# Sparse first FFN of a macaron block: routing by whole rows, blocks in plain f32, router stationary, weight stores in an early tick

## The chip, the cores and the metric

The kernel runs on one core of one Trainium2 chip. The metric is the device time of one execution in microseconds, as the median of three runs; lower is better. Times inside the kernel are read from one profiled execution, counted from the start of its span.

## What is computed

The reference is a macaron block on x of shape 8 x 1024 x 256 in f32: a mixture-of-experts FFN, an attention, and the same FFN again (same weights), each behind a layer norm and added to x (the FFNs at half weight).

```python
x = x + 0.5 * ffn(layernorm(x))      # the "first FFN": all of the change is here
x = x + attn(layernorm(x))           # window attention + 256 routed tokens of each row
x = x + 0.5 * ffn(layernorm(x))

def ffn(x):                          # 8 experts, top 2, hidden width 128
    w = softmax(x @ router_w + router_b)
    w2, i2 = top_k(w, 2);  w2 = w2 / sum(w2)
    h = gelu(x @ W1[e] + b1[e])      # 256 -> 128
    return sum over the two of w2 * (h @ W2[e] + b2[e])
```

## The kernel before

"Row" means one of the 8 batch rows of 1024 tokens (8 tiles of 128 tokens); a "group" is half a row (4 tiles), 16 groups in all.

**The first FFN is sparse.** For each group, `group_stats`, `rstd` (with an index of 0), `group_norm` normalise the tokens; `group_turn` transposes them with TensorE (8 transposes, line 812); `group_logits` makes the router's logits with the tokens as the stationary operand (line 822); `group_route` ranks the experts on VectorE; `group_spots` counts places (TensorE, lines 830 and 832, then VectorE); `exp2nd_a` and `group_gates` give the two weights. Then `send` on GpSimd (line 1889) scatters every token tile twice, once for each of its two experts, to `spots_d` in HBM: 8 indirect DMAs a group, 128 in all. Rows are taken in three batches, (0,1), (2,3,4), (5,6,7). When all tokens of a batch lie at their places, SyncE writes pads (`pads`, line 590, 8 DMAs of 256 KB), and the batch is worked off in blocks of 256 tokens of one expert: 23, 31 and 31 blocks, 85 "steps".

**A step** is `block_load` (line 602, 256 KB), `block_turn` (4 transposes, line 842), `block_hi` and `block_lo` (ScalarE line 1148 and VectorE line 1504: the value split in a rounded part and a rest, both fp32r), `w1_copy` (ScalarE, the expert's W1 in both parts), `block_hidden` (6 fp32r matmuls of 256 columns), `block_gelu` (ScalarE, twice: lines 1157 and 1158), `block_hl` (GpSimd line 1893: the rest of h), `block_out` (6 fp32r matmuls of 256 columns), `block_left` (VectorE line 1516, bias), `block_store` (line 608, 256 KB). `mm3` (lines 717 to 719) makes the product of two split operands by three fp32r matmuls.

**The order is written by hand in ticks.** Every engine runs through the same ticks and does what falls in each in program order; an engine that waits holds all its later ticks. Step s starts in tick 24 + s; `block_hidden` is 2 ticks later, `block_out` 5, `block_store` 7. Groups start at ticks `GROUP_AT`, sends are 8 to 11 ticks later, two in a tick. In the third batch's ticks row 0 of the attention is prepared: `fetch` gathers its results, then `combine`, norms and transposes.

**After the ticks** come "slots" of the attention (40 for a row) and then the second FFN, dense; these also use the split weights, which are stored to HBM (`w1_d`, `w2_d`, `b2_d`, 4 MB, line 660) in tick 90 and read back near the end. The three last projections of the change's region, `qkv` of row 0, run in the last ticks.

Of the kernel before, what the change touches and what calls it, by code (L numbers as in the profile page):

```python
# [8 lines left out]
F32 = mybir.dt.float32  # L9
# [9 lines left out]
P = 128  # L19
# [16 lines left out]
BLK = 256  # L36


def build(nc, x_in, gamma_h, wq_h, wkv_h, wo_h, ln_g, ln_b, wqkv, wo_l, rt_q, rt_kv,
# [22 lines left out]
    MAXM = 4 * T * max(r1 - r0 for r0, r1 in BATCH) // 2  # L62
# [7 lines left out]
    with ctx:  # L70
# [56 lines left out]
        home = sb("home", [P, GROUPS, 2, TG], U32)  # L127
        share = sb("share", [P, GROUPS, 2, TG])
# [21 lines left out]
        w2_st = at("w2_st", [P, E, D], F32, yr_off + n1 * 4)  # L150
# [32 lines left out]
        chosen = [sb(f"chosen{i}", [P, TG + 1, E], BF16) for i in range(2)]  # L183
        lg = sb("lg", [P, TG, E])
        lrank = sb("lrank", [P, TG, E])
        l2nd = sb("l2nd", [P, TG, E])
        cmp_g = sb("cmp_g", [P, TG, E, E], BF16)
        cmp_e = sb("cmp_e", [P, TG, E, E], BF16)
        run = sb("run", [P, E])
        sums = sb("sums", [P, TG, E])  # L190
        picks = sb("picks", [P, 2, TG, E])

        spot_f = sb("spot_f", [P, GROUPS, 2, TG])
        spot = sb("spot", [P, GROUPS, 2, TG], U32)
# [14 lines left out]
        xin = [sb(f"xin{i}", [P, BT, D]) for i in range(4)]  # L209
        w1_s = sb("w1_s", [P, E, 2, C, FF], F32R)  # L210
        w1_now = [sb(f"w1_now{i}", [P, 2, C, FF], F32R) for i in range(2)]
        w2_s = [sb("w2_hi", [P, E, D], F32R), sb("w2_lo", [P, E, D], F32R)]
        assert top[0] >= z2 + (HC * N + HC * PADDED + (T + 1) * INNER) * 4
        b2_s = sb("b2s", [64 + E, D], F32R)

        wqkv_st = at("wqkv_st", [P, C, 3 * INNER], F32, top[0])
        b2_st = at("b2_st", [E, D], F32, top[0] + n3 * 4)
        hf = [sb(f"hf{i}", [P, BLK]) for i in range(NH)]
        hl = [sb(f"hl{i}", [P, BLK], F32R) for i in range(NH)]
        hh = [sb(f"hh{i}", [P, BLK], F32R) for i in range(NH)]  # L220
        yout = [sb(f"yout{i}", [P, BT, D]) for i in range(4)]
        block_e = [sb(f"block_e{n}", [P, MAXB], I32) for n in range(len(BATCH))]
        block_row = [sb(f"block_row{n}", [P, MAXB], I32) for n in range(len(BATCH))]
        pad_row = [sb(f"pad_row{n}", [P, E], I32) for n in range(len(BATCH))]
        assert top[0] <= xf_off, (top[0], xf_off)

        xb_off = [xt_off + i * TG * D * 4 for i in range(4)] + [y_off, y_off + TG * D * 4] + [yr_off + (T * (D + 1) + i * TG * D) * 4 for i in range(2)]
        xb = [at(f"xb{i}", [P, TG, D], F32, off) for i, off in enumerate(xb_off)]
        zeros = at("zeros", [P, BT, D], F32, xt_off + 4 * TG * D * 4)
        assert 4 * TG * D + BT * D <= 2 * C * PADDED  # L230
        x_off = [x1_off + T * D * 4, x1_off + (T * D + 2 * C * BLK) * 4, yr_off]
        xh = [at(f"xh{i}", [P, C, BLK], F32R, x_off[i]) for i in range(3)]
        xl = [at(f"xl{i}", [P, C, BLK], F32R, x_off[i] + C * BLK * 4) for i in range(3)]
# [41 lines left out]
        s_xa, s_sc = [sem(f"xa_ld{i}") for i in range(8)], [sem(f"sent{i}") for i in range(8)]  # L275
        s_ax, s_ra, s_exa, s_pos, s_tab, s_zero = sem("xa_turned"), sem("route_a"), sem("exp2_a"), sem("spots"), sem("table"), sem("pads")
        s_home, s_b2all = sem("homes"), sem("b2_all")

        s_bld, s_bst = [sem(f"block_ld{i}") for i in range(4)], [sem(f"block_st{i}") for i in range(4)]
        s_bT, s_bhi, s_blo, s_w1c, s_bh = sem("block_turned"), sem("block_hi"), sem("block_lo"), sem("w1_copied"), sem("block_hidden")  # L280
        s_bge, s_bhl, s_bo, s_by, s_spare = sem("block_gelu"), sem("block_h_lo"), sem("block_out"), sem("block_y"), sem("spare_zero")
# [37 lines left out]
        def group_at(tau, after):  # L319

            return [k for k, t in enumerate(GROUP_AT) if t + after == tau]
# [8 lines left out]
        def batch_of_group(k):  # L330
            return [n for n, (r0, r1) in enumerate(BATCH) if r0 <= k // 2 < r1][0]

        def last_of_batch(k):
            return k == 2 * BATCH[batch_of_group(k)][1] - 1
# [14 lines left out]
        QKV0 = {STEP0 + STEPS + 3 + i: i for i in range(3)}  # L349
# [139 lines left out]
        def left(job):  # L489

            kind, x, i = job
            if kind == "aT":
                return s_ax, 2 * x + i + 1
# [63 lines left out]
        def sent(engine, n):  # L557

            for k in range(2 * BATCH[n][0], 2 * BATCH[n][1]):
                engine.wait_ge(s_sc[k % 8], 128 * (k // 8 + 1))  # L560
# [8 lines left out]
        def sp_program():  # L569
# [7 lines left out]
            def group_load(k):  # L577
                if k in (6, 7):

                    sp.wait_ge(s_wlo, 4)  # L580
                if k >= 8:
                    sp.wait_ge(s_sc[k % 8], 128 * (k // 8))
                sp.dma_start(xb[k % 8][:, :, :], half(x_v, k)).then_inc(s_xa[k % 8], 16)
# [40 lines left out]
            group_load(0)  # L624
            sp.dma_start(rw_st[:, :, :], router_w.rearrange("(c p) n -> p c n", p=P)).then_inc(s_wld[0], 16)
            group_load(1)
# [3 lines left out]
            group_load(2)  # L630
            group_load(3)
            for tau in range(TICKS):
                for s_ in step_at(tau - 7):
                    block_store(s_)
                for s_ in step_at(tau + 3):
                    block_load(s_)
                for k in group_at(tau + 6, 0):
                    if k >= 4:
                        group_load(k)
                if tau == 7:  # L640
                    sp.dma_start(wqkv_st[:, :, :], wqkv.rearrange("(c p) n -> p c n", p=P)).then_inc(s_wld[4], 16)
                if tau == 11:
                    sp.dma_start(b2_all[:, :, :].rearrange("p e n -> p (e n)"), b2.rearrange("(a e) n -> a (e n)", a=1).broadcast_to([P, E * D])).then_inc(s_b2all, 16)
                if tau in (13, 36, 60):

                    if tau == 13:
                        sp.wait_ge(s_const, CONST)
                    n = (13, 36, 60).index(tau)
                    sp.dma_start(spots_d[n][SPARE[n]:SPARE[n] + (E - 1) * BLK, :].rearrange("(j p s) d -> p j (s d)", p=P, s=BT),
                                 zeros[:, :, :].rearrange("p s d -> p (s d)").unsqueeze(1).broadcast_to([P, E - 1, BT * D])).then_inc(s_spare, 16)  # L650
                if tau == 82:
                    sp.dma_start(wqh_s[:, :, :], wq_h.rearrange("(c p) n -> p c n", p=P)).then_inc(s_late, 16)
                    sp.dma_start(wkvh_s[:, :, :], wkv_h.rearrange("(c p) n -> p c n", p=P)).then_inc(s_late, 16)
                if tau == 86:
                    sp.dma_start(wol_s[:, :, :], wo_l.rearrange("(c p) n -> p c n", p=P)).then_inc(s_late, 16)
                    sp.dma_start(woh_s[:, :, :], wo_h.rearrange("(c p) n -> p c n", p=P)).then_inc(s_late, 16)
                if tau == 90:
# [6 lines left out]
                if tau == 70:  # L664
                    attn_load(0, x_v)
            sp.wait_ge(s_bh, STEPS)
# [48 lines left out]
        def pe_program():  # L715
# [11 lines left out]
            def ffn_turn(k, pr):  # L727
                pe.wait_ge(s_norm[0], 2 * (GROUPS + k) + pr + 1)
# [77 lines left out]
            def group_turn(k, pr):  # L806
# [8 lines left out]
            def group_logits(k):  # L815
                pe.wait_ge(s_ax, 2 * k + 2)
                if k == 0:
                    pe.wait_ge(s_wld[0], 16)
# [1264 lines left out]
```

## Time and profile before

| | us |
|---|---|
| median of 3 runs | 2117.42 (2114.1 to 2122.3) |
| profiled execution | 2120.96, its span 2119.2 |
| busy in the span | PE 1892.2, VectorE 1473.1, ScalarE 1214.2, GpSimd 1208.1 |
| mean granted TensorE clock | 0.969 |
| first block load of the three batches | 86.75, 183.36, 288.07 |
| last block store issued | 393.1 |

How to read it: the first FFN takes the time up to about 393 us and the change touches nothing behind that. So what moves the time is when the last step is done. Busy shares over the whole span say little here, since attention and second FFN (four fifths of the time) run behind other limits.

### The profile page before, as it was taken

The page shows a single profiled execution, that of the slowest core. Times are in us where ns is not written, and L with a number is a line of the kernel's source. Part 1 is how long each engine was busy: PE and PEld are TensorE (multiplying, and loading weights), DVE is VectorE, ACT ScalarE, POOL GpSimd, SP SyncE. Part 2 cuts the span into 40 slices and gives each one's busy share as a digit, 9 for nine tenths or more (in the row PEclk, how much of TensorE's full clock was granted, in tenths as well). Part 3 has the DMA queues.
Part 4 walks back from the last instruction along what each step waited for, and adds up shares of the span by engine and source line. Part 5 has one row for each costly group of instructions (what it writes and reads, how often), then busy time and mean ns, then how long its engine had stood idle before and what let it go on. Part 6 is the DMA issues. An engine that isn't in the chain of part 4 may idle for free.

```text
span 2119.2 us, 39516 instructions
## 1 busy us (share of the span) xinstructions
PE 1892.2 (89%) x12240; PEld 1458.9 (69%) x12240; DVE 1473.1 (70%) x5026; ACT 1214.2 (57%) x3005; POOL 1208.1 (57%) x1376
## 2 busy tenths in 40 slices
PE   4568877888998998998998998998999999999998
PEld 4567766655665665665665665665676688888887
DVE  5566856765684685685684684685665488888887
ACT  4356757646556556556556556556555555555554
POOL 6887855284386386385385386386364444444444
PEclk9978988989999999999999999999999999999999
DMA  7567887320031031030030031031023111111110
GB/s 251 172 223 264 269 301 258 119 74 12 6 103 28 8 101 29 9 103 26 20 91 26 9 100 28 9 100 29 4 58 115 37 41 41 39 34 39 40 33 29
DMA packets 106695, 173.74 MB, mean 82 GB/s; under 512 B 13408, under 2 KB 65016, under 8 KB 105592
## 3 DMA queue, kind: packets, MB, share of 16 engines
q1 hardware_dynamic: 83448, 118.42, 17.0%
q0 software_dynamic: 20736, 52.52, 8.0%
q8 instruction: 101, 1.65, 0.3%
q10 hardware_dynamic: 2304, 0.28, 0.2%
q14 instruction: 106, 0.87, 0.1%
HBM read 80.33 MB, written 90.84 MB: 81 GB/s over the span
## 4 chain that ended last, share of the span: by engine, by line
PE 45%; DVE 17%; POOL 12%; issue 11%; ACT 8%; DMA 5%; SPq 1%; DVEq 0%; ACTq 0%; POOLq 0%
PE bank L717 8%; PE bank L719 6%; PE bank L718 6%; PE bank L1000 4%; PE bank L989 4%; PE bank L960 4%; PE bank L971 4%; PE bank L931 3%; POOL spots_d L1889 3%; ACT prob L1277 2%; DVE st L1366 2%; POOL prob L1940 2%; DVE x L1529 2%; DMA z_row<-made_d,home 2%; PE bank L962 1%
## 5 line engine op out<-in xcount | busy, mean ns | idle before, releaser
L1940 POOL TENSOR_TENSOR prob<-prob,rden 128x512 f32<-128x512 f32 x320 | 338.0, 1057 | 456.1 <-DVE rden L1735 452.5
L1277 ACT ACTIVATE prob<-prob,nmax 128x256 f32<-128x256 f32 x512 | 255.9, 502 | 404.1 <-DVE nmax L1717 404.1
L1717 DVE CUSTOM_DVE_ANT_0 prob<-bank,mask 128x256 f32<-128x256 f32 x512 | 195.3, 418 | 103.6 <-PE bank L960 102.5
L1604 DVE SCALAR_TENSOR_TENSOR xb<-bank,gate,xb 128x256 f32<-128x256 f32 x512 | 211.8, 476 | 55.5 <-PE bank L719 54.7
L960 PE MATMUL bank<-kT,qT 64*128 64x256 f32 x1024 | 212.5, 433 | 22.8 <-DVE nmax L1717 22.2
L1865 POOL TENSOR_TENSOR hl<-hf,hh 128x512 fp32r<-128x512 f32 x128 | 164.9, 1294 | 113.4 <-ACT hh L1098 108.8
L971 PE MATMUL bank<-ident,prob 128*128 128x128 f32 x1280 | 199.6, 279 | 19.6 <-POOL prob L1940 19.6
L971 PEld LDWEIGHTS bank<-ident,prob 128*128 128x128 f32 x1280 | 155.0, 143 | 78.5 <-POOL prob L1940 31.0
L1729 DVE COPY probT<-bank 128x512 f32<-128x512 f32 x160 | 110.1, 688 | 120.6 <-PE bank L971 119.8
L1097 ACT ACTIVATE hf<-bank,b1s 128x512 f32<-128x512 f32 x128 | 88.2, 689 | 171.6 <-PE bank L719 168.1
L989 PE MATMUL bank<-probT,V 128*64 128x128 f32 x2048 | 170.2, 287 | 8.2 <-ACT oT_s L1293 6.6
L1927 POOL DMA_INDIRECT hs_d<-yr,place x128 | 130.0, 1016 | 43.6 <-issue 32.3
L960 PEld LDWEIGHTS bank<-kT,qT 64*128 64x128 f32 x1024 | 94.4, 187 | 86.7 <-issue 44.1
L989 PEld LDWEIGHTS bank<-probT,V 128*64 128x64 f32 x2048 | 108.6, 137 | 63.5 <-issue 61.4
L717 PE MATMUL bank<-w,hh 128*128 128x256 f32 x512 | 146.0, 285 | 3.9 <-POOL hl L1865 2.7
L1889 POOL DMA_INDIRECT spots_d<-xb,spot x128 | 127.6, 997 | 34.2 <-issue 32.2
L719 PE MATMUL bank<-w,hh 128*128 128x256 f32 x512 | 144.5, 282 | 0.0
L718 PE MATMUL bank<-w,hl 128*128 128x256 f32 x512 | 144.2, 282 | 0.0
L1000 PE MATMUL bank<-wol,oT_s 128*128 128x256 f32 x512 | 127.3, 392 | 1.2 <-ACT xf_t L1224 1.2
L1749 DVE TENSOR_TENSOR x<-bank,x 128x256 f32<-128x256 f32 x64 | 27.0, 423 | 145.1 <-PE bank L1000 145.1
L717 PE MATMUL bank<-xt_hi,wqkv_hi 128*128 128x512 f32 x256 | 115.5, 451 | 0.0
L1000 PEld LDWEIGHTS bank<-wol,oT_s 128*128 128x128 f32 x512 | 93.0, 191 | 24.1 <-issue 13.8
(254 smaller groups left out, 5461.5 us busy)
## 6 DMA issues: line engine op xcount, KB each, us to landing
xin<-spots_d SPq DMA_DIRECT2D x85, 256.0 KB, 4.1
made_d<-yout SPq DMA_DIRECT2D x85, 256.0 KB, 3.7
xb<-in_L_attn_x SPq DMA_DIRECT2D x16, 512.0 KB, 6.3
x<-in_L_attn_x SPq DMA_DIRECT2D x8, 1024.0 KB, 6.5
x_d<-x SPq DMA_DIRECT2D x8, 1024.0 KB, 4.5
xb<-x_d SPq DMA_DIRECT2D x16, 512.0 KB, 3.8
out<-xb SPq DMA_DIRECT2D x16, 512.0 KB, 2.9
spots_d<-zeros SPq DMA_DIRECT2D x24, 256.0 KB
```

Of the source, the lines that this page charges most:

```text
L717: pe.matmul(o, w[0], x[0], start=start, stop=False)
L718: pe.matmul(o, w[1], x[0], start=False, stop=False)
L719: return pe.matmul(o, w[0], x[1], start=False, stop=stop)
L960: ins = pe.matmul(bank[g % NS][:, 0:KEYS], qT[hs, hp, t * P:(t + 1) * P], kT[hs, hp, t * P:t * P + KEYS], start=True, stop=True)
L971: ins = pe.transpose(bank[3 + j % 2][:, (2 * h + kk) * P:(2 * h + kk + 1) * P], prob[j % NP][:, h, kk * P:(kk + 1) * P], ident[:, :])
L989: ins = pe.matmul(bank[5][h * DH:(h + 1) * DH, hp * P:(hp + 1) * P], V[:, t + kk, hs] if t < T else hv[:, kk, hs], probT[j % 2][:, 2 * h + ...
L1000: ins = pe.matmul(bank[tb][:, 0:D], oT_s[:, ch, :], w[:, ch, :], start=(ch == 0), stop=(ch == HC - 1))
L1277: act.activation(prob[j % NP][:, h, :], src, ACT.Exp, bias=nmax[:, j % 4, h:h + 1], scale=-1.0 if light else 1.0, accum_out=den[:, j % 4, ...
L1604: dve.scalar_tensor_tensor(out=x, in0=bank[ob][:, (t % 2) * D:(t % 2 + 1) * D], scalar=gate[:, k % 2, t, e:e + 1], in1=x, op0=ALU.mult, op ...
L1717: ins = dve.tensor_tensor_reduce(prob[j % NP][:, h, :], bank[g % NS][:, 0:KEYS], mask[:, which, :], -1.0, 3e38, ALU.add, ALU.min, nmax[:, ...
L1889: pool.indirect_dma_start(spots_d[batch_of_group(k)], bass.IndirectOffsetOnAxis(spot[:, k, c, q:q + 1], 0), xb[k % 8][:, q, :], None).then ...
L1940: pool.tensor_tensor(prob[j % NP][:, :, :], prob[j % NP][:, :, :], rden[:, j % 4, :].unsqueeze(2).broadcast_to([P, 2, KEYS]), ALU.mult).th ...
```

## The change

Four edits, with the ticks laid out anew around them.

1. Routing by whole rows: `row_stats`, `row_rstd`, `row_norm`, `row_turn`, `row_route`, `row_exp`, `row_gates`, `row_spots` take 8 tiles at a time, each with half as many instructions on operands of twice the width; the number of sends stays at 128, three in a tick. Rows start at ticks `ROW_AT`; the load of a row is one DMA of 1 MB (row 0 in two halves).
2. The blocks in plain f32: no split of x, h or the weights, so `block_lo`, `block_hl` and one of the two gelus go, `w1_copy` copies half as much, and `block_hidden` and `block_out` have 2 plain matmuls each for 6. The pipeline of a step is two ticks shorter.
3. Logits with the router stationary: 4 matmuls of 512 columns into 8 partitions for a row (`row_logits`), copied by ScalarE and turned back by 8 small transposes.
4. The splits of the weights (still needed by attention and second FFN) move from ticks 2 to 19 to ticks 8 to 25; the store of the split weights moves from tick 90 to tick 18, the loads of the attention's late weights from ticks 82 and 86 to 100 and 106.

```diff
-        STEP0 = 24
-        TICKS = STEP0 + STEPS + 8
-        GROUP_AT = (0, 3, 6, 9, 12, 15, 18, 22, 26, 30, 36, 41, 46, 51, 56, 61)
+        STEP0 = 26
+        TICKS = STEP0 + STEPS + 6
+        ROW_AT = (0, 6, 12, 19, 26, 36, 46, 56)
...
-            jobs = [("aT", k, pr) for k in group_at(tau, 3) for pr in range(2)]
-            jobs += [("alg", k, 0) for k in group_at(tau, 4)]
-            jobs += [("apos", k, 0) for k in group_at(tau, 6)]
+            jobs = [("aT", r, i) for i in range(4) for r in row_at(tau, 4 + i // 2)]
+            jobs += [("alq", r, i) for r in row_at(tau, 6) for i in range(2)]
+            jobs += [("alg", r, 0) for r in row_at(tau, 7)]
+            jobs += [("apos", r, 0) for r in row_at(tau, 9)]
...
-                if tau == 90:
+                if tau == 18:
                     sp.wait_ge(s_wlo, 6)
                     sp.dma_start(w1_d, ...)
...
+                for c in range(C):
+                    ins = pe.matmul(bank[tb][0:E, :], rw_st[:, c, :], xa[h][:, c, :], start=(c == 0), stop=(c == C - 1))
...
+                for t in range(T):
+                    ins = pe.transpose(bank[tb][:, t * E:(t + 1) * E], lgT[t // TG][:, t % TG * P:(t % TG + 1) * P], ident[0:E, 0:E])
...
                 for c in range(C):
-                    ins = mm3(bank[2 + s_ % 2][:, 0:BLK], [w1_now[s_ % 2][:, n, c, :] for n in range(2)], [x[s_ % 3][:, c, :] for x in (xh, xl)],
-                              start=(c == 0), stop=(c == C - 1))
+                    ins = pe.matmul(bank[2 + s_ % 2][:, 0:BLK], w1_now[s_ % 2][:, c, :], xh[s_ % 3][:, c, :], start=(c == 0), stop=(c == C - 1))
...
                 for j in range(BT):
-                    cs = slice(j * P, (j + 1) * P)
-                    ins = mm3(bank[4 + s_ % 2][:, j * D:(j + 1) * D], [hh[s_ % NH][:, cs], hl[s_ % NH][:, cs]], w, start=True, stop=True)
+                    ins = pe.matmul(bank[4 + s_ % 2][:, j * D:(j + 1) * D], hf[s_ % NH][:, j * P:(j + 1) * P], w, start=True, stop=True)
...
-                act.activation(hf[s_ % NH][:, :], bank[2 + s_ % 2][:, 0:BLK], ACT.Gelu, bias=b1_e)
-                act.activation(hh[s_ % NH][:, :], bank[2 + s_ % 2][:, 0:BLK], ACT.Gelu, bias=b1_e).then_inc(s_bge)
+                act.activation(hf[s_ % NH][:, :], bank[2 + s_ % 2][:, 0:BLK], ACT.Gelu, bias=b1_s[:, bass.ds(e_act[s_], 1)]).then_inc(s_bge)
...
                 for s_ in step_at(tau):
                     block_turn(s_)
-                for s_ in step_at(tau - 5):
+                for s_ in step_at(tau - 3):
                     block_out(s_)
-                for s_ in step_at(tau - 2):
+                for s_ in step_at(tau - 1):
                     block_hidden(s_)
...
-                for s_ in step_at(tau - 4):
-                    block_hl(s_)
-                for k in group_at(tau, 1):
-                    rstd(0, k, 2 * k)
-                for k in group_at(tau, 6):
-                    exp2nd_a(k)
-                for i in range(8):
-                    for k in group_at(tau, 8 + i // 2):
-                        send(k, i)
+                for r in row_at(tau, 2):
+                    row_rstd(r)
+                for r in row_at(tau, 9):
+                    row_exp(r)
+                for i in range(2 * T):
+                    for r in row_at(tau, 11 + i // 3):
+                        send(r, i)
```

## Rows read from the trace of the kernel before

**Rows 1.** Windows: us; busy (count) PE, PEld, DVE, ACT, POOL; clock, DMA share, GB/s.

```profile
86.75:183.36 96.61, 71.84 (x471) 68.38 (x471) 62.75 (x201) 58.07 (x119) 79.72 (x99) 0.84 0.70 235
183.36:288.07 104.71, 81.14 (x617) 77.26 (x617) 76.86 (x205) 69.81 (x149) 76.84 (x96) 0.90 0.81 272
288.07:393.50 105.43, 83.10 (x567) 76.00 (x568) 65.55 (x147) 74.00 (x161) 59.98 (x86) 0.89 0.76 261
393.50:2119.20 1725.70, 1615.44 (x10389) 1201.31 (x10387) 1217.05 (x4256) 980.94 (x2521) 929.63 (x995) 0.98 0.15 45
```

**Rows 2.** Timeline of SyncE's queue: start, us, instruction, count.

```profile
86.75 2.81 SPq L602 DMA_DIRECT2D xin<-spots_d  x4
...
172.44 8.01 SPq L590 DMA_DIRECT2D spots_d<-zeros  x8
183.36 0.36 SPq L602 DMA_DIRECT2D xin<-spots_d  x1
...
288.07 0.35 SPq L602 DMA_DIRECT2D xin<-spots_d  x1
...
331.28 0.46 SPq L660 DMA_DIRECT2D w_d<-w_s  x1
```

**Rows 3.** Groups of GpSimd, 86.75 to 183.36: busy, mean ns, idle before, releaser.

```profile
L1889 POOL DMA_INDIRECT spots_d<-xb,spot x52 | 51.3, 987 | 14.5 <-issue 12.7 <-DVE spot L1450 1.7
L1893 POOL TENSOR_TENSOR hl<-hf,hh 128x256 fp32r<-128x256 f32 x20 | 15.2, 764 | 0.9 <-ACT hh L1158 0.5
L1840 POOL TENSOR_TENSOR tri<-tri,cols 128x4 f32<-128x4 f32 x5 | 5.3, 1070 | 0.0
```

**Rows 4.** What TensorE waited for: groups, 86.75 to 393.5; then waits, 86.75 to 183.36.

```profile
L842 PE MATMUL bank<-ident,xin 128*128 128x128 f32 x340 | 61.9, 313 | 43.9 <-DMA xin<-spots_d 25.7 <-DVE xl L1504 18.1
L717 PE MATMUL bank<-w_hi,hh 128*128 x170 | 60.5, 356 | 20.3 <-POOL hl L1893 16.7 <-issue 1.6 <-DVE yout L1516 1.0
...
PE bank L717 <- POOL hl L1893: 10.1, 2, 7.8
PE bank L842 <- DVE xl L1504: 6.7, 5, 4.1
```

**Rows 5.** Timeline of TensorE in an undisturbed tick of the third batch.

```profile
381.49 0.60 PE L842 MATMUL bank<-ident,xin 128*128 128x128 f32 x4
...
382.16 0.28 PE L719 MATMUL bank<-w_lo,hh 128*128 x1
382.28 0.28 PE L717 MATMUL bank<-w_hi,hh 128*128 x1
...
383.35 0.60 PE L842 MATMUL bank<-ident,xin 128*128 128x128 f32 x4
```

**Rows 6.** Timeline of TensorE in the attention: plain f32 matmuls of 256 columns.

```profile
813.10 1.99 PE L1000 MATMUL bank<-wol,oT_s 128*128 128x256 f32 x8
814.93 0.49 PE L971 MATMUL bank<-ident,prob 128*128 128x128 f32 x3
```

**Rows 7.** Timeline of ScalarE in the same ticks.

```profile
382.32 0.46 ACT L1157 ACTIVATE hf<-bank,b1s 128x256 f32<-128x256 f32 x1
...
384.18 0.46 ACT L1157 ACTIVATE hf<-bank,b1s 128x256 f32<-128x256 f32 x1
```

**Rows 8.** Timeline of TensorE's jobs for one group of tokens.

```profile
230.05 1.03 PE L812 MATMUL bank<-ident,xb 128*128 128x128 f32 x8
...
232.78 1.85 PE L822 MATMUL bank<-rw_st,xa 128*128 128x8 f32 x16
```

**Rows 9.** Windows around one stall, columns as in rows 1.

```profile
110.00:115.00 5.00, 0.48 (x2) 0.49 (x3) 0.00 (x0) 3.79 (x8) 4.43 (x6) 0.50 0.52 187
115.00:120.00 5.00, 5.00 (x28) 5.00 (x28) 3.49 (x13) 1.42 (x3) 4.09 (x5) 0.55 0.30 105
120.00:125.00 5.00, 5.00 (x47) 5.00 (x45) 3.29 (x7) 3.41 (x9) 4.40 (x5) 1.00 0.56 198
```

**Rows 10.** The chain of waits, 0 to 480: the first send and the last wait for one.

```profile
28.97 1.23 POOL spots_d L1889
...
83.67 2.40 DMA spots_d<-xb,spot
```

More of the change, by code:

```diff
@@ L61, in build @@
     STEPS = sum(BLOCKS)
-    MAXM = 4 * T * max(r1 - r0 for r0, r1 in BATCH) // 2
+    MAXM = 2 * T * max(r1 - r0 for r0, r1 in BATCH)
     MAXB, MAXI = max(BLOCKS), max(r1 - r0 for r0, r1 in BATCH) * N // BLK
@@ L557, in sent @@
         def sent(engine, n):
-            for k in range(2 * BATCH[n][0], 2 * BATCH[n][1]):
-                engine.wait_ge(s_sc[k % 8], 128 * (k // 8 + 1))
+            for r in range(*BATCH[n]):
+                engine.wait_ge(s_sc[r % 4], 32 * T * (r // 4 + 1))
         def made(engine, n):
@@ L833, in group_spots, with row_spots @@
+            def row_spots(r):
+                pe.wait_ge(s_ra, NA * r + 9)
+                tb = claim(("apos", r, 0))
+                m = chosen[r % 2]
+                pe.matmul(bank[tb][:, 0:(T + 1) * E], later[:, :], m[:, :, :].rearrange("p t e -> p (t e)"), start=True, stop=False)
+                for d in range(1, T + 1):
+                    ins = pe.matmul(bank[tb][:, d * E:(T + 1) * E], ones[:, :], m[:, 0:T + 1 - d, :].rearrange("p t e -> p (t e)"), start=False, stop=(d == T))
                 ins.then_inc(s_full)
@@ new lines, in row_stats @@
+            def row_stats(r, h):
+                if h == 0 and r == 0:
+                    dve.wait_ge(s_xa0, 16)
+                else:
+                    dve.wait_ge(s_xa[r % 4], 16 * (r // 4 + 1))
+                for q in range(TG * h, TG * h + TG):
+                    ins = dve.bn_stats(st_a[:, q, :], xb[r % 4][:, q, :])
+                ins.then_inc(s_abn)
+                dve.wait_ge(s_abn, 2 * r + h + 1)
+                if h == 0 and r > 0:
+                    dve.wait_ge(s_avar, 2 * r)
+                for q in range(TG * h, TG * h + TG):
+                    ins = dve.bn_aggr(mv_a[:, q, :], st_a[:, q, :])
+                ins.then_inc(s_amv)
@@ L1774, in dve_program @@
-                if tau == 7:
+                for h in range(2):
+                    for r in row_at(tau, h):
+                        row_stats(r, h)
+                for r in row_at(tau, 10):
+                    row_spots(r)
+                    if last_of_batch(r):
+                        batch_table(batch_of_row(r))
+                    row_gates(r)
+                for r in row_at(tau, 8):
+                    row_route(r)
+                for r in row_at(tau, 12):
+                    if last_of_batch(r):
+                        batch_homes(batch_of_row(r))
@@ new lines, in row_exp, with send @@
+            def row_exp(r):
+                pool.wait_ge(s_ra, NA * r + 11)
+                pool.tensor_tensor(t2nd_a[:, :], euler_a[:, :], t2nd_a[:, :], ALU.pow).then_inc(s_exa)
+            def send(r, i):
+                t, c = divmod(i, 2)
+                if i == 0:
+                    pool.wait_ge(s_pos, NPOS * (r + 1))
+                    pool.wait_ge(s_anorm, 4 * r + 4)
+                pool.indirect_dma_start(spots_d[batch_of_row(r)], bass.IndirectOffsetOnAxis(spot[:, r, c, t:t + 1], 0), xb[r % 4][:, t, :], None).then_inc(s_sc[r % 4], 16)
```

417 lines of the change are left out of this document (201 added, 216 removed).

## The prediction

> **What bounds the kernel now.** I read the windows first [rows 1]: only the first FFN is touched, and what follows 393.5 us (1725.7 us) stays as it is. So the question is how much earlier or later the last block store comes. The loads in SyncE's queue [rows 2] cut the region: a front up to 86.75 us in which nothing but routing runs, then batch 0 (A, 96.6 us, 23 steps), batch 1 (B, 104.7 us, 31 steps) and batch 2 up to the last store (C, 105.4 us, 31 steps).
>
> In the front the chain of waits runs over GpSimd's sends [rows 10]: from the first at 28.97 us to the landing that ends at 86.07. In A GpSimd is full: 52 sends cost 51.3 us busy and 12.7 us issue, so 1.23 us each, and `hl` and the small ones fill the rest; 79.7 us busy and 14.5 us beside the sends leave 2 of 96.6 us [rows 1, 3]. A step needs its `hl`, so sends and steps share one queue.
>
> TensorE is the second bound, and the one to watch. An undisturbed tick is 1.86 us: from one `block_turn` to the next, with 12 fp32r matmuls 0.12 us apart, 1.42 us, and 0.44 for the transposes [rows 5]. ScalarE's tick there is 1.86 us as well [rows 7]. The jobs of a group cost 0.9 (8 transposes), 1.85 (logits) and about 0.45 (places) = 3.2 us [rows 8]. By its ticks, A holds 23 steps and 4.5 groups: 42.8 + 14.4 = 57.2 us of TensorE at full clock; B 31 and 4.5: 57.7 + 14.4 = 72.1; C 31 steps, the turns of row 0 and three projections (6) and the drain (5): 68.7. Sum 198. The three stretches last 306.7, so 109 us are "excess": waits and slow clock, 39.4 in A, 32.6 in B, 36.7 in C.
>
> **What the excess is made of.** TensorE waited 25.7 us for block loads, 18.1 for `xl` and 16.7 for `hl` [rows 4]. The rest is mostly the clock: it was 0.84, 0.90 and 0.89 [rows 1], and after one wait for `hl` of 7.8 us [rows 4] it stood at 0.50 to 0.55 for 10 us, with 28 instructions in 5 us at full occupation where the next 5 us, at 1.00, hold 47 [rows 9]. So at the lower level (1.2 for 2.4 GHz) work costs twice, and each long wait is paid twice.
>
> **The change part by part.**
> *Plain f32 in the blocks.* In the attention 4 plain matmuls of 256 columns (8 records) run from 813.10 to 814.93 [rows 6]: 1.83 us for what a step will have, against 1.42 for its 12 fp32r ones. A tick becomes 0.44 + 1.83 = 2.27 us: **+0.41, times 85 = +35 us** of TensorE work. The other engines gain: VectorE loses `xl`, GpSimd `hl` (0.76 us each) [rows 3], ScalarE one gelu and half a copy, to about 1.2 us a tick. These alone are worth nothing; what they are worth is waits that vanish. The Trainium skill, "FP8 and Floating Point Precision", TensorE Precision Notes, has true FP32 at four passes through the array; at 0.118 us a pass this would be 1.89 us, a tick of 2.33 and +40 us. The row is from this kernel, so I take 1.83. It speaks against the change all the same: three products become four passes.
>
> *Whole rows.* Per row TensorE has 16 transposes (1.8), 4 plain matmuls of 512 columns (8 records at twice 0.23: 3.6), 8 small transposes (0.8) and places (0.9): 7.1 against 2 x 3.2 = 6.4, so the new logits save nothing. I bound them by 1.8 (the columns cost as in an fp32r matmul) and 7.3 (slow clock). GpSimd's small work halves: one pow of 1.07 us [rows 3] serves 8 tiles; a wider one from 1.07 (fixed) to 2.1 (twice): I take 1.1. VectorE's route becomes one lump of about 5 us in place of two of 3.3, below a tick pair of 4.5.
>
> *The front.* The first send needs the whole of row 0: twice the norms and transposes, then the logits. I put it at 35 us (33 to 40) instead of 29. Then 32 sends at 1.23 to 1.27 with some 9 us of norms and pows of rows 1 to 3 end at about 84, with 2.4 us to land [rows 10]: 86.6, where it was 86.75. **0** (-3 to +4).
>
> *A.* GpSimd needs 48 x 1.25 + 3 x 3.5 = 71 us for rows 2 to 4 and no longer bounds the steps. TensorE: 23 x 2.27 + 2.3 rows x 7.1 = 68.5. Excess: 39.4, less `hl` and `xl` (10.1 + 6.7) [rows 4] and 6 of slow clock behind the long one = 16.6. It keeps waits of ScalarE and VectorE for `row_rstd` and `row_exp`, which stand behind up to 16 sends. 85 us, **-11.5**.
> *B.* 31 x 2.27 + 2 x 7.1 = 84.6; excess 32.6 less 7.4 of waits less 3 of clock = 22. 107, **+2**. Here GpSimd was only partly the limit, and the larger tick eats all.
> *C.* 31 x 2.27 + 10 = 80.4; excess 36.7 less 10.5 less 2 of clock, less 3.6 for the weight stores, which at 331.28 [rows 2] put 4 MB before the block loads = 20.6. 101, **-4.5**. The 7.4 and 10.5 are my split of the 18.0 us of the two waits that do not lie in A.
> *Moved DMAs.* The stores now go out in tick 18, when VectorE has made the splits; SyncE has row 4's load and the first pads behind them, both of which wait for GpSimd or for tick 23, some 20 us later: nothing. If that cover is gone, 4 MB at the 235 to 272 GB/s of rows 1 are 16 us. The late weights (2.5 MB) now go out in ticks 100 and 106, beside the last block loads: 0 to +3, I take 0; attention needs them 20 slots later. The splits at ticks 8 to 25 lie in the front: 0, and +3 if they hold `w1_copy` of step 0, which waits for them.
>
> **Sum.** 0 - 11.5 + 2 - 4.5 = **-14 us**: 2121.0 becomes 2107; the profiled execution stood 3.5 us above its median, so I forecast **2104**. In one line: +35 of TensorE work, -49 of excess (109 to 60). 0.5% is 10.6 us, about what a measurement of this kernel can tell from no change.
>
> **Rivals.**
> *TensorE keeps its waits (slower).* If the waits for `xl` and `hl` only change their name (to loads, to `row_rstd`), the +35 stands. It decides as soon as less than 35 of the 109 us goes. For it: loads are already TensorE's largest wait [rows 4]; with 261 to 272 GB/s at a share of 0.76 to 0.81 [rows 1] faster steps meet fuller DMA queues. Against: 34.8 us of waits have their very producer removed. With 20 us gone: 2132; with none: 2152. Chance 0.15.
> *No difference.* 25 to 45 us of excess go. DMA is the likely holder. 306.7 us at a share of about 0.76 are 233 us of full transfers, 13 to 16 less without the stores: no floor, but longer landings. The time: 2113 or so. Chance 0.28.
> *Clock stays up.* If TensorE, fuller by a fifth, waits for loads alone (25.7) and is slow for 10, excess falls to 36: -38, 2080. The clock fell behind a wait and rose under full work [rows 9]; fewer waits and more work per tick would keep it up. Chance 0.17. The Trainium skill, "TensorE: Matmul & The Clock Gate", HAM oscillation, tells the same mechanism: waits throttle the array, activity releases it; the rows agree with it.
> *The forecast*, excess down by 45 to 60: 2093 to 2108. Chance 0.40.
>
> So faster by over 0.5%: 0.17 and nearly all of the forecast, 0.55; within: 0.30; slower: 0.15. The range leaves out the worst half of the first rival and the best tail of the third: 2080 to 2127.
>
> **What would show it.** Records of `block_hidden` and `block_out` 0.23 apart and ticks of 2.27 us; first send at 35 us, first block load near 87, then near 172, 278; last store near 379; no wait for `xl` or `hl`; clock above 0.9 in A. Wrong if the first load slips past 92, if waits for block loads grow beyond 40 us, if VectorE's lump or waits for `row_rstd` and `row_exp` exceed 15 us of TensorE's time, or if the attention changes.

## The result

The changed kernel takes 2144.42 us (median of 4, 2143.86 to 2147.52) against 2116.61 (four runs, the three of the table above among them): **1.0131 times the time before, interval 1.0114 to 1.0149. It is slower by 1.3%**, clear of the noise, where 2104 was forecast, and above the range of 2080 to 2127. The profiled execution spans 2142.2 us. All of it lies in the first FFN: what follows the last block store takes 1724.6 us (1725.7 before).

Windows of the changed kernel, the same stretches as [rows 1]: batch 0 (A), batch 1 (B), batch 2 to the last block store (C).

```profile
core 0: us, PE busy (x) PEld busy (x) DVE busy (x) ACT busy (x) POOL busy (x), PEclk, DMA share, GB/s
86.88:203.26 116.38, 76.08 (x366) 52.87 (x363) 44.96 (x149) 47.04 (x100) 61.53 (x66) 0.82 0.58 197
203.26:325.99 122.73, 93.58 (x454) 71.54 (x454) 40.21 (x107) 55.08 (x121) 48.97 (x55) 0.88 0.69 231
325.99:417.65 91.66, 79.59 (x410) 67.72 (x411) 44.66 (x114) 54.94 (x125) 32.73 (x51) 0.93 0.73 246
```

The front came out as forecast (first load 86.88). A is 19.8 us longer and B 18.0, C 13.8 shorter: +24 in all. VectorE, ScalarE and GpSimd lost the work they were to lose (VectorE in A 62.8 to 45.0, GpSimd 79.7 to 61.5 against [rows 1]), the DMA share fell as well, and still A and B grew: no other engine got fuller, and the engines stand idle for longer. TensorE's undisturbed tick is 2.17 us, from one `block_turn` (L853, here at 361.79, the one before at 359.62) to the next. `block_out` (L877) and `block_hidden` (L862) lie between:

```profile
360.06 1.03 PE L877 MATMUL bank<-w_st,hf 128*128 x4
360.92 1.03 PE L862 MATMUL bank<-xh,w_now 128*128 128x256 f32 x4
361.79 0.60 PE L853 MATMUL bank<-ident,xin 128*128 128x128 f32 x4
362.22 1.03 PE L877 MATMUL bank<-w_st,hf 128*128 x4
```

So the blocks have 0.31 x 85 = 26 us more TensorE work than before. With a tick of 2.17 us in place of 2.27 the prediction's sum of ticks and rows' jobs comes to 225 us. The stretches last 330.8: the excess is 106 us, where it was 109 and was to become 60.

**Where it stands.** An engine that has done a piece of work updates a semaphore, a counter for which the next engine waits; the trace has the time of each such update. The view of waits (from 86 to 400 us: engine, line, releaser, total, times, longest) has a kind that the trace of the kernel before doesn't have at all, "remote": waits whose release the profile can put down to no engine and no DMA of the kernel.

```profile
DVE yout L1538 <- remote: 71.5, 8, 13.4
ACT xa L1136 <- remote: 28.1, 7, 9.3
ACT xh L1149 <- remote: 24.5, 4, 15.0
ACT hf L1170 <- remote: 15.4, 3, 10.1
DVE lg L1422 <- remote: 12.6, 1, 12.6
```

Together 152 us, on VectorE and ScalarE at once. The timeline of the first of them (start, us, engine, line, operation, idle before and releaser):

```profile
90.23 0.66 PE L833 MATMUL bank<-ident,lgT 8*128 8x8 f32 x8
90.82 0.66 PE L853 MATMUL bank<-ident,xin 128*128 128x128 f32 x4
91.33 0.40 ACT L1164 ACTIVATE w_now<-w_st 128x256 f32 x1
91.58 1.10 PE L862 MATMUL bank<-xh,w_now 128*128 128x256 f32 x4
...
95.24 0.96 POOL L1923 DMA_INDIRECT spots_d<-xb,spot  x1 [0.30 <-issue]
96.51 0.96 POOL L1923 DMA_INDIRECT spots_d<-xb,spot  x1 [0.30 <-issue]
...
103.18 0.22 DVE L1422 TENSOR_TENSOR lg<-bank,rbs 128x64 f32<-128x64 f32 x1 [12.63 <-remote]
...
106.72 0.60 ACT L1149 ACTIVATE xh<-bank 128x512 f32<-128x512 f32 x1 [14.98 <-remote]
```

`lg` waits for nothing but the 8 turns of L833, which end at 90.9, and starts at 103.18. `xh` of step 1 waits for the 4 transposes at 90.82 and starts at 106.72. The recorded updates of the semaphores agree with these starts: that of L833 is at 103.16, those of `block_turn` 1 and 2 and of `block_hidden` 0 at 106.69, 106.81 and 106.75. Updates that belong to 91 to 94 us come in one set, 0.06 us apart. Over the first FFN 47 updates of TensorE's are recorded more than 0.7 us after the latest work that they can tell of, 311 us in sum (a lower bound, since some updates are missing from the record); in the trace of the kernel before none is, and none of VectorE's, ScalarE's or GpSimd's in either. The common standstills with such waits begin 8 us or more into a stretch of 13 to 19 sends (or, in the third batch, 14 fetches) that GpSimd issues without a pause (79.9 to 103.8, 111.4 to 130.0, 159.9 to 176.2 and so on, 1.27 us apart); the kernel before has pairs of sends with `hl` between from 111 us on, and up to there stretches of at most 8. Windows across the first standstill (columns as above):

```profile
91.00:95.00 4.00, 2.23 (x12) 1.33 (x11) 0.00 (x0) 0.73 (x2) 3.02 (x4) 1.00 0.63 169
95.00:99.00 4.00, 0.00 (x0) 0.00 (x0) 0.00 (x0) 0.00 (x0) 2.87 (x3) 0.74 0.53 174
99.00:103.00 4.00, 0.00 (x0) 0.00 (x0) 0.00 (x0) 0.00 (x0) 3.06 (x4) 0.50 0.40 151
```

Three engines do nothing, the DMA share falls to 0.40 and the granted clock to 0.50, the lower of its two levels. Stretches in which VectorE, ScalarE and TensorE all do nothing for over 1.2 us come to 49 us between 86 and 430 us (56 from 60 on); before, to 8.

### The profile page after: what moved, and what is told of

Same layout as the page of the kernel before. It is cut to its first block, busy times and chain, and to the rows that moved or that the text cites. A ratio compares the mean times of both kernels' runs of the same rounds, so it can differ in the third digit from the quotient of the medians.

```text
span 2142.2 us, 37969 instructions
## 1 busy us (share of the span) xinstructions
PE 1899.1 (89%) x11764; PEld 1409.7 (66%) x11764; DVE 1389.8 (65%) x4781; ACT 1175.3 (55%) x2936; POOL 1126.9 (53%) x1253
## 3 DMA queue, kind: packets, MB, share of 16 engines
q1 hardware_dynamic: 83336, 118.42, 16.7%
## 4 chain that ended last, share of the span: by engine, by line
PE 46%; DVE 16%; issue 13%; POOL 12%; ACT 8%; DMA 2%; another core or an unknown queue 1%; SPq 1%; DVEq 0%; ACTq 0%; POOLq 0%
PE bank L720 6%; PE bank L722 5%; PE bank L721 5%; PE bank L1009 4%; PE bank L998 4%; PE bank L969 4%; PE bank L980 4%; PE bank L940 3%; POOL spots_d L1923 3%; ACT prob L1292 2%; POOL prob L1970 2%; DVE x L1550 2%; DVE st L1381 2%; PE bank L971 1%; PE bank L877 1%
## 5 line engine op out<-in xcount | busy, mean ns | idle before, releaser
L980 PEld LDWEIGHTS bank<-ident,prob 128*128 128x128 f32 x1280 | 153.9, 142 | 79.9 <-POOL prob L1970 33.3
L1538 DVE TENSOR_TENSOR yout<-bank,b_all 128x512 f32<-128x512 f32 x85 | 58.0, 690 | 174.4 <-remote 71.5
L877 PE MATMUL bank<-w_st,hf 128*128 x340 | 97.0, 411 | 21.3 <-issue 13.6
```

The costliest lines, as they stand in the source:

```text
L980: ins = pe.transpose(bank[3 + j % 2][:, (2 * h + kk) * P:(2 * h + kk + 1) * P], prob[j % NP][:, h, kk * P:(kk + 1) * P], ident[:, :])
```

## The experiments

Theory R: long unpaused stretches of sends hold back other engines' semaphore updates. Theory L: whole rows make long lumps in queues that run in order, and plain f32 adds to them; the sends only happen to run meanwhile. The runs came in five sets, each on a chip of its own (P, Q, S, T, U here), where the kernel before took 2116.35, 2114.60, 2121.07, 2113.91 and 2114.35 us. "Remote" below is the sum of those waits from 86 to 400 us.

### First set: chip P

**e1_paced**: GpSimd waits for the steps before its sends.

```diff
+                for s_ in step_at(tau - 3):
+                    pool.wait_ge(s_bge, s_ + 1)
                 for i in range(2 * T):
```

> The new kernel with one wait added on GpSimd: in tick tau it waits for the gelu of step tau-3 before it goes on to its three sends, as the old kernel's hl did; no work is added or left out. In the trace of the new kernel GpSimd issues 13 to 19 sends without a pause, and from some 8.5 us into each such stretch VectorE, ScalarE, TensorE and SyncE stand still together, 49 us in all between 60 and 430 us (8 in the old kernel), several times with what they wait for already done. Theory R (long unbroken stretches of sends hold the other engines): sends come in threes, the common standstill falls under 15 us and the time to 2100 to 2120. Theory L (the lumps of whole rows, the in-order queues and the f32 passes cost the time; the sends only happen to run meanwhile): a further wait can only hurt, 2140 to 2165.

2130.23 us, 1.0070 (1.0045 to 1.0094), remote 123. With a wait added it is some 14 us faster than the changed kernel (2144.42, on another chip), which L excludes; but 2130 is above R's band. The trace shows that the wait did not part the sends: stretches of 12 to 19 stay, probably because GpSimd is behind the steps there and finds the wait met.

**e2_breaks**: a clear of 128x4 after every second send.

```diff
                         send(r, i)
+                        if i % 2:
+                            ...
+                            pool.memset(t2nd[:, TG:2 * TG], 0.0).then_inc(s_gap)
```

> The new kernel with an own operation of GpSimd between sends: after every second send it clears 4 unused columns (128x4), 64 of them in all, and waits for nobody else. Sends are still not paced by the steps. R in its weak form (any other instruction of GpSimd breaks the stretch): as the paced one, 2100 to 2120, with standstills under 15 us. R in its strong form (GpSimd has to pause, or the sends are too dense over 10 to 20 us): standstills stay near 49 us, 2144 plus up to 64 x 0.2 = 13 us, so 2140 to 2158. L: 2144 to 2158 too.

2151.24 us, 1.0188 (1.0157 to 1.0218), remote 153. An operation of 0.12 us after each pair changes nothing. That fits strong R or L.

**e3_early**: the kernel before, stores in tick 18 instead of 90.

```diff
-                if tau == 90:
+                if tau == 18:
```

> The kernel before with edit 4 alone: the weight stores (4 MB) go out in tick 18 instead of tick 90. If the last batch's gain in the new kernel (105.4 to 91.7 us) comes from this edit: 2117 less 10 to 14, 2103 to 2107. If it comes from the lighter steps: 2113 to 2119. If the 4 MB hold up the front's sends and loads: slower, up to 16 us, 2120 to 2133.

2111.49 us, 0.9988 (0.9971 to 1.0005): no difference from the kernel before that can be told from none, and between the first two bands. C falls from 105.4 to 101.6, 3.8 us, the 3.6 of the prediction; no harm in the front. Remote is 3.4, in 2 waits. This is the only trace of the old routing, with its sends in pairs, from a chip on which updates come late: here too 19 updates of TensorE's are over 0.7 us late, but by 26 us in sum, and the two latest (3.9 and 3.6 us, at 109.3 and 110.8 us) stand at the end of its one stretch of 8 sends.

**e4_tokens**: the changed kernel with the old form of the logits.

```diff
-            jobs += [("alq", r, i) for r in row_at(tau, 6) for i in range(2)]
...
+                for t in range(T):
+                    for c in range(C):
+                        ins = pe.matmul(bank[tb][:, t * E:(t + 1) * E], xa[t // TG][:, c, t % TG * P:(t % TG + 1) * P], rw_st[:, c, :], start=(c == 0), stop=(c == C - 1))
```

> The new kernel with the logits made as before (16 matmuls of 8 columns with the tokens stationary, one job a row, no copy of the logits by ScalarE and no turn back). If the router-stationary logits (5 to 6.5 us of TensorE in a cold stretch, two copies of 0.59 us on ScalarE, one more hand-over) cost their price on the path: 5 rows x 2 to 4 us less, 2124 to 2134. R: they lie inside stretches that the sends hold up anyway, 2138 to 2148. L: 2124 to 2140, since the row's lump gets smaller.

2163.24 us, 1.0227 (1.0198 to 1.0256): both theories missed. The old form costs more, not less, in this frame: 52.0 us of TensorE for 8 rows against 40.2 + 5.3 (matmuls and the turn back), in the same window from 20 to 430 us:

```profile
L835 PE MATMUL bank<-rw_st,xa 128*128 128x8 f32 x256 | 52.0, 346 | 2.1 <-ACT xa L1138 1.4 <-issue 0.7
```

and of the changed kernel:

```profile
L826 PE MATMUL bank<-xa,rw_st 128*8 128x512 f32 x64 | 40.2, 786 | 15.6 <-issue 8.8 <-ACT xa L1136 6.8
L833 PE MATMUL bank<-ident,lgT 8*128 8x8 f32 x64 | 5.3, 204 | 2.0 <-ACT lgT L1143 2.0
```

That it also keeps `xa` longer and puts a row's jobs in one lump behind the steps may add to it; no run parts these. The router-stationary form is not what lost the time.

### Second set: chip Q

**e5_pow**: as e2_breaks, with a pow in place of the clear.

```diff
-                            pool.memset(t2nd[:, TG:2 * TG], 0.0).then_inc(s_gap)
+                            pool.tensor_tensor(t2nd[:, TG:2 * TG], euler[:, :], minus_half[:, :], ALU.pow).then_inc(s_gap)
```

> The kernel of the run before with breaks, with one thing exchanged: the own operation after every second send is a pow on 4 unused columns (1.04 us in the profile) in place of the clear of the same 4 columns (0.1 us). It adds 64 us of work to GpSimd, on results that nobody reads. Theory R, strong form (it takes a real pause in the sends of about 1 us, as the old hl gave, for TensorE's semaphore updates to get through): the recorded updates of TensorE's semaphores, which come 2 to 14 us late and then 0.06 us apart in all runs of the new kernel with 13 to 19 sends in a row, come on time (late by under 2 us), the common standstill falls from 56 us to under 20, and in spite of the 64 us the time falls below the 2151 of the clear: 2110 to 2135. Theory L (lumps and queues): GpSimd becomes longer by 64 us where TensorE already waits for its row_rstd and row_exp: 2160 to 2200.

2113.99 us, 1.0002 (0.9985 to 1.0019), remote 0, in R's band: 64 operations that nobody needs, over 64 us of GpSimd, and 30 us less than the changed kernel's 2144.42 on another chip. It looked like the proof of R. It was not. The three other kernels of chip Q have long stretches of sends and no late update either, so there was probably nothing here for the pows to mend; on chip U below, which has no late update, the changed kernel without them takes 2085.40.

**e6_onepass**: block matmuls as one fp32r pass.

```diff
-        w1_now = [sb(f"w1_now{i}", [P, C, FF]) for i in range(2)]
+        w1_now = [sb(f"w1_now{i}", [P, C, FF], F32R) for i in range(2)]
...
-                w = w2_st[:, bass.ds(e, 1), :].rearrange("p a n -> p (a n)")
+                w = w2_s[0][:, bass.ds(e, 1), :].rearrange("p a n -> p (a n)")
```

> The new kernel with the block matmuls as one fp32r pass on rounded values instead of plain f32: the low parts are left out of the first FFN's blocks. The sends, the queues and the routing stay as they are. TensorE's tick falls from 2.17 to about 1.0 us, 85 x 1.2 = 100 us less of its work. If the heavier TensorE tick (the +35 of the prediction) sets the time: 2080 to 2105. If TensorE mostly stands in stretches where its semaphore updates are held, and ScalarE's tick of about 2 us is next: the standstills stay (over 35 us) and the time falls little, 2115 to 2138.

2068.78 us, 0.9791 (0.9768 to 0.9813), remote 0, below both bands. Its sends still run 13 to 19 in a row, and no update is late. That does not fit R as it stood.

**e7_copy** and **e8_copy2**: the copy of a step's w1 on GpSimd; e8_copy2 has two sends a tick besides.

```diff
+                for s_ in step_at(tau):
+                    w1_copy(s_)
...
-                    for r in row_at(tau, 11 + i // 3):
+                    for r in row_at(tau, 11 + i // 2):
```

> The new kernel with the copy of a step's w1 (128x256 f32, once a tick) on GpSimd in place of ScalarE. It lies between the sends of one tick and the next, about 0.8 us like the old hl, and waits for block_hidden two steps back, so it paces GpSimd as well. R: no stretch of more than 3 to 6 sends, updates on time, standstills under 15 us, 2095 to 2118; ScalarE is 0.42 us a tick lighter. L: one more chain through GpSimd's queue (block_hidden waits for the copy behind three sends): 2140 to 2170.

> The same with two sends a tick instead of three, so a row's 16 sends take 8 ticks: the very rhythm of the old kernel. R: as e7 or better in the updates, but batch tables some 3 ticks later: 2095 to 2120. L: 2140 to 2170.

2103.50 us, 0.9950 (0.9930 to 0.9970), in R's band, and 2094.50 us, 0.9897 (0.9862 to 0.9932), just below it; remote 0 in both. The copy takes 0.40 us and leaves a pause of 0.6 between pairs. Stretches of 13 to 16 sends stay in the front and up to 97 us, where GpSimd is behind the steps, and no update is late beside them either.

### Third set: chip S

**e9_repeat**: e6_onepass with each block matmul issued four times.

```diff
-                for c in range(C):
+                for c in [0, 1] * 4:
...
-                for j in range(BT):
+                for j in [0, 1] * 4:
```

> The one-pass kernel of the run before, with every block matmul of it issued four times over (the same operands, the result of the last stands): 16 fp32r matmuls a step. TensorE is then as busy as with plain f32 (16 x about 0.12 = 1.9 us beside the 0.44 of transposes), in a kernel without plain f32 in the blocks; low parts are left out. In the one-pass kernel no update of TensorE's semaphores was late although 13 to 19 sends stood in a row, so long stretches of sends are not enough by themselves. If the second condition is a TensorE that is kept full (theory W): late updates come back, 100 us or more in sum, and with the standstills 2125 to 2150. If it is the plain f32 matmuls themselves (theory F): no update is late by over 2 us, and the time is that of a tick of 2.3 us without standstills, 2095 to 2120.

2166.20 us, 1.0220 (1.0193 to 1.0248), remote 176, updates late by 346 us in sum: theory W (a full TensorE is the second condition) had the sign right, F fell, and the time is above both bands. The rest of this set spoke against W.

**e10_mix**: e8_copy2 with three sends a tick for rows 0 and 1.

```diff
-                    for r in row_at(tau, 11 + i // 2):
-                        send(r, i)
+                    for r in range(ROWS):
+                        if ROW_AT[r] + 11 + i // (3 if r < 2 else 2) == tau:
+                            send(r, i)
```

> The new kernel with the w1 copy on GpSimd and two sends a tick, but three a tick for rows 0 and 1, since two a tick put the first block load from 86.9 to 92.0 us. If the front's delay is all that it cost: first load at 87 to 88.5 and 2094.5 less 3 to 5, 2088 to 2092. If the copy's place in GpSimd's queue sets it: no change, 2093 to 2096.

2105.13 us, 0.9934 (0.9913 to 0.9955). The first load is at 87.03 as expected, yet the time is above both bands, and remote is 83 us where e8_copy2 had 0. The chip is enough to account for that: e8_copy2 itself is at 0.9933 with 74 us on chip T below. What the edit does by itself, these runs can't tell.

**e11_light**: e8_copy2 in one pass (the edits of e6_onepass).

> The kernel with the w1 copy on GpSimd and two sends a tick, with the blocks in one fp32r pass (low parts left out). With the sends held apart in both, the difference to 2094.5 is what plain f32 costs by TensorE's work alone. By the ticks it is 85 x 1.2 = 100 us at most; if TensorE's passes bound the steps: 2094.5 less 40 to 60, 2035 to 2055; if ScalarE's tick and GpSimd's queue are next and bound the steps at about 2 us: 2070 to 2085.

2093.43 us, 0.9882 (0.9848 to 0.9917), above both bands, remote 91: TensorE is light and updates are late all the same. W falls here.

**e12_bursts**: the kernel before, a row's 16 sends in one stretch.

```diff
-                for i in range(8):
-                    for k in group_at(tau, 8 + i // 2):
-                        send(k, i)
+                for k in group_at(tau, 8):
+                    if k % 2:
+                        for i in range(16):
+                            send(k - 1 + i // 8, i % 8)
```

> The kernel before (12 fp32r matmuls a step) with the 16 sends of a row issued in one stretch, after the row's second group, instead of two a tick; hl stands behind them in GpSimd's queue, so it will be slower in any case (a step waits up to 20 us for hl: 2140 to 2180). What it is to tell is in the recorded updates of TensorE's semaphores: theory W or a rule on the sends alone: late by 5 us and more in these stretches, in sets 0.06 us apart. Theory F: only small lateness (under 4 us), about the f32 transposes and logits.

2184.55 us, 1.0314 (1.0284 to 1.0344), 5 above the band, remote 128, and 38 updates late by 305 us in sum, up to 17 us. So plain f32 in the blocks isn't needed. The run is 63 us slower than the kernel before. How much of that comes from late updates and how much from `hl` behind the sends, it can't say.

### Fourth and fifth set: chips T and U

What set chip Q apart was not in its kernels: their four traces hold 84 to 86 updates of each block semaphore (85 steps) and about 19,800 updates in all, and the first trace of the kernel before is as complete (20,283). The traces of the changed kernel and of the first and third set hold 60 to 82 for nearly every block semaphore, and 15,100 to 16,100 in all. So three of chip Q's kernels and the changed one, all as they were, went to another chip together.

> The new kernel, unchanged, beside the next three on one chip. If long stretches of sends hold TensorE's updates everywhere: 1.013 of the kernel before, 2140 to 2148, on any chip. If it is a matter of the chip: on a chip whose trace has no late update it is at 2105 to 2120, the same as before or faster, and the copies below gain less on it than 50 us; on one with late updates 2140 to 2150.

> The kernel with 64 pows of 1.04 us between sends again, on another chip. If the pause in the sends does it: 2110 to 2125 again and no update late by over 2 us. If the chip did it: on a chip with late updates GpSimd's 64 us come on top, 2150 to 2200.

> The one-pass kernel (low parts left out) again, on another chip. If a TensorE that is not full is safe from late updates: 2065 to 2080 and none late by over 2 us. If the chip did it: late updates appear beside its 13 to 19 sends in a row, 2085 to 2110.

> The kernel with the w1 copy on GpSimd and two sends a tick again, on another chip. If its rhythm does it: 2090 to 2100 again, 50 us under the new kernel beside it. If the chip did it: 2110 to 2145, or little under the new kernel's time on the same chip.

Chip T was one on which updates are held back.

| kernel | us | to the kernel before (interval) | remote | late updates, in sum | same kernel on Q or U |
|---|---|---|---|---|---|
| changed kernel (f1_same) | 2142.75 | 1.0135 (1.0111 to 1.0158) | 154 | 327 | 2085.40 (U) |
| pow after each pair (f2_pow) | 2123.33 | 1.0045 (1.0027 to 1.0062) | 20 | 31 | 2113.99 (Q) |
| one pass (f3_onepass) | 2119.82 | 1.0031 (1.0015 to 1.0047) | 133 | 282 | 2068.78 (Q) |
| w1 copy, pairs (f4_copy2) | 2101.05 | 0.9933 (0.9912 to 0.9954) | 74 | 92 | 2094.50 (Q) |

f1_same and f2_pow lie in their first bands, though with the pow 6 updates are late, by up to 8 us. These, and its 3 remote waits, all stand at the end of the 14 fetches in a row, between which no pow stands. f3_onepass has the late updates that were expected if the chip did it, and is 10 us above that band. f4_copy2 is 42 us under the changed kernel, not 50. f3_onepass has the very instructions of e6_onepass and is 51 us slower. The same place in both, first on chip Q:

```profile
90.86 0.22 DVE L1422 TENSOR_TENSOR lg<-bank,rbs 128x64 f32<-128x64 f32 x1 [1.12 <-PE bank L833]
90.90 0.58 ACT L1149 ACTIVATE xh<-bank 128x512 fp32r<-128x512 f32 x1
```

and on chip T, where the turns of L833 end at 92.6:

```profile
103.33 0.22 DVE L1422 TENSOR_TENSOR lg<-bank,rbs 128x64 f32<-128x64 f32 x1 [11.94 <-remote]
```

Then the changed kernel once more, alone:

> The new kernel, unchanged, on whatever chip this call gets. On a chip with late updates: 2140 to 2148 once more. On a chip without: the one-pass kernel lost 51 us to the late updates, and the copies with the w1 copy 7 us; if the new kernel loses what its standstills beyond those of the kernel before come to (41 us) and something for the clock behind them: 2095 to 2108, the forecast; if its in-order waits and heavier ticks fill the same stretches anyway: 2115 to 2135.

On chip U no update is late: **2085.40 us (2083.26 to 2089.33, 4 runs), 0.9863 (0.9839 to 0.9886) of the kernel before**, 19,843 updates, remote 0, with the same stretches of 13 to 19 sends. Its windows:

```profile
87.26:174.01 86.75, 69.78 (x366) 51.01 (x364) 45.19 (x149) 46.22 (x100) 61.05 (x66) 0.91 0.77 265
174.01:275.85 101.84, 88.39 (x454) 69.46 (x454) 40.37 (x107) 55.38 (x121) 49.16 (x55) 0.92 0.82 278
275.85:360.00 84.15, 79.39 (x414) 68.14 (x415) 44.68 (x114) 55.38 (x126) 32.86 (x51) 0.94 0.81 271
```

The time is below all bands, under the forecast too. The last block store ends at 359.1. Against the windows of the first section the counts of A and B are the same, the busy times of VectorE, ScalarE and GpSimd nearly so; the clock is 0.91 and 0.92 for 0.82 and 0.88 in A and B, and the common standstills from 86 to 430 us come to 16 us for 49. One program is 59 us apart (2144.42 and 2085.40) where the kernel before differs by 2 (2116.61 and 2114.35).

## Why the prediction was wrong

The step that failed is the one from the waits to the excess, "109 to 60". It had the waits that vanish and those that the parts of the kernel give each other, but no term for updates that reach the waiting engines up to 15 us late beside a long stretch of sends. Where they came late the excess went from 109 to 106, with 152 us of remote waits of VectorE and ScalarE (partly at the same time). Where no update was late (chip U) the excess did fall, below the forecast: 271.8 us of stretches less 225 of TensorE work is 47. There TensorE's waits came to 35 us, 15.9 of them for loads and 9.7 for `yout`; before they were 72, with 25.7 for loads, 18.1 for `xl` and 16.7 for `hl`. In numbers, us:

| term | forecast | changed kernel | on chip U |
|---|---|---|---|
| first send | 35 | 35.07 | 33.68 |
| first block load | 86.6 | 86.88 | 87.26 |
| TensorE, blocks | +35 | +26 | +26 |
| A | -11.5 | +19.8 | -9.9 |
| B | +2 | +18.0 | -2.9 |
| C | -4.5 | -13.8 | -22.1 |
| excess | 60 | 106 | 47 |
| time | 2104 | 2144.4 | 2085.4 |

- **Plain f32**: 2.17 us a tick for 2.27, a term mis-sized by 9 us. The matmul's records stand 0.216 us apart, the attention's 0.23 [rows 6]. The new logits cost what was said: 18.0 us for 5 rows on chip U, 3.6 a row. "FP8 and Floating Point Precision" of the Trainium skill (TensorE Precision Notes), by its four passes, gave an estimate of 2.33, too much by 0.16; the measurement decides. What the passes cost in time is far less than their work: without late updates the changed kernel is at 0.9863 (chip U) and the one-pass kernel at 0.9791 (chip Q), 0.7% or 15 us, for 75 us of busy TensorE in the three stretches (237.6 and 162.9).
- **Front**: right, the first send and the first load.
- **A and B** hold to 2 and 5 us on chip U. GpSimd stopped being A's bound, as said (61.1 of 86.8 us busy). The 2104 is 19 us above chip U's time because the tick and the excess were both put too high; on the other chips these two errors are hidden under the missing term.
- **C**: mis-sized everywhere, by 9 and by 18 us. The stores were 3.8 of it, as forecast (e3_early). The rest is waits: TensorE waited 24.1 us in C before (11.7 for loads, 5.6 `hl`, 4.9 `xl`, 1.9 gelu) and 7.8 on chip U. The prediction took the loads' part as given, but two of its three waits went as well:

```profile
PE bank L853 <- DMA xin<-spots_d: 6.1, 1, 6.1
PE bank L877 <- ACT hf L1170: 0.9, 3, 0.4
PE bank L877 <- DVE yout L1538: 0.6, 1, 0.6
```

- **Rivals.** "TensorE keeps its waits" came near the time (2152 with none of the excess gone; 3 of 109 went), by luck, since its mechanism was wrong: waits for `xl` and `hl` didn't change their name to loads or `row_rstd`, TensorE's own updates came late. "Clock stays up" (2080) is what chip U shows: 0.91 to 0.94 and an excess of 47. The prediction's signs of error, above 15 us lost to the lump or to `row_rstd` and `row_exp`, named the place (16 sends in one queue) but priced it at a part of 16.6 us, as a wait of others for GpSimd's own small operations, which is another mechanism.

**What is shown**: late updates go with long stretches of sends and with the chip. On chip T a pow of about 1 us after each pair takes remote from 154 to 20 us and the time from 2142.75 to 2123.33 in spite of 64 us more work; sends in stretches of 16 bring them in full into the kernel before (e12_bursts, 305 us late in sum, against 26 in e3_early). Of the five kernels on chips Q and U none has late updates, though four have stretches of 13 to 19 sends. A full TensorE and plain f32 in the blocks aren't conditions. That the 57 to 59 us between chips are the late updates' is argued: the counts and the other engines' busy times agree, and what differs in the windows is idle time, the clock and the DMA rate. No run moved the updates and nothing else.

**What stays open**: why chips differ. The traces with late updates are the very ones that lack about a fifth to a quarter of their update records, so the taking of records may itself be what is held. The Trainium skill, "NOTIFIC — the notification-queue block" (Overflow: three behaviours, one of which stalls the engine), has a rule of that kind: a record queue that is full can stall the engine that writes to it. The traces agree in that loss and lateness come in the same traces, and they don't agree further. On chip P the kernel with the old routing lacks a fifth of its records (16,069) and takes no longer than elsewhere, and after the last block store the changed kernel's first trace lacks 1,500 of chip U's 12,500 and lasts 1724.6 us for 1722.6. Most of what is missing are updates by landed DMAs (6,981 for 11,056). And each timed execution here comes with a span and a clock of its own, so records were taken in all, and no run shows a time without them. Nor was it tried whether a given chip always behaves one way. The late weight loads were not moved alone.

**The better version.** On a chip where no update is late the changed kernel as it is (0.9863) is ahead of all that keep its arithmetic; the next, 0.9897, has an interval that overlaps. Where updates come late, the w1 copy on GpSimd with two sends a tick is at 0.9933 and the changed kernel at 1.0135. The copy's kernel is at 0.9897 on chip Q, so it is ahead of the kernel before on both kinds of chip.

## What to carry to other kernels

When several engines stand at once and what they wait for is done by the profile, don't look for a lump in a queue: compare the times of semaphore updates with the ends of the instructions that make them. Run the same program on a second chip, and the unchanged kernel beside every variant, before an idle time gets a mechanism: e5_pow looked like a proof because the kernel that it was held against had run on another chip. Operations of an engine that look like a cost (`hl` on GpSimd) can be what keeps its DMA issues apart; ask what a queue does when such an operation goes.

## What the runs showed of the hardware

- TensorE's semaphore updates can come up to 17 us after the matmul (e12_bursts; 15 in the changed kernel) and then in sets 0.06 us apart, beside GpSimd's indirect DMAs issued every 1.27 us; the DMA share is then 0.40 to 0.53. No update of another compute engine is late.
- SyncE slows down at these places too. From 87.6 to 98.9 us of the changed kernel its instructions, whatever they are, start 0.70 to 0.72 us apart or twice that, and some take 0.70 us instead of 0.04 to 0.34. Between 60 and 430 us 25 of its instructions take 0.69 to 0.71 us, on chip U 1.
- The same program takes 2142.75 us on one chip and 2085.40 on another, on which the kernel before differs by 0.44 us (2113.91, 2114.35).
- A 128x4 clear on GpSimd takes 0.12 us and a 128x4 pow 1.03 to 1.08; a 128x8 pow 1.65 to 1.77 (means of groups), so the wider pow costs 0.6 us more, where the prediction had taken 1.1 us for it.
- A 128x256 copy is 0.40 us on GpSimd, as on ScalarE (0.40 to 0.42).
